# Graph layer on one core: second layer of the inner pairs in split products with the weights standing, ring of six rounds

## The reference

```python
def reference(x, src, dst, edge_attr_128, W1, b1, W2, b2):
    h = jnp.maximum(_layernorm(x, axis=-1), 0.0)
    # edge features are summed by node; the sums and h are concatenated
    agg = jax.ops.segment_sum(edge_attr_128, dst, num_segments=6250)
    z = jnp.concatenate([agg, h], axis=1)           # 6250 x 256
    hidden = jax.nn.relu(z @ W1 + b1)               # W1: 256 x 512
    return x + hidden @ W2 + b2                     # W2: 512 x 128
```

## Time and profile before

| | us |
|---|---|
| median of 3 runs | 201.23 |
| the profiled execution | 201.16 |
| its span (first to last instruction) | 199.3 |
| PE busy | 190.6 (96%) |
| DVE busy | 131.8 (66%) |
| ACT busy | 86.5 (43%) |
| POOL busy | 43.4 (22%) |
| mean of the 16 DMA engines, over the span | 313 GB/s |

### The profile page before, as it was taken

The page is one execution under the profiler, slowest core; times in us unless marked ns, Lnnn a source line. Parts: engine busy times, 40 slices in busy tenths (PEclk is TensorE's granted clock), DMA queues, the critical chain, the costliest instruction groups (busy, mean ns, idle before and its releaser), DMA issues.

```text
span 199.3 us, 6821 instructions
## 1 busy us (share of the span) xinstructions
PE 190.6 (96%) x2568; PEld 163.2 (82%) x2568; DVE 131.8 (66%) x582; ACT 86.5 (43%) x188; POOL 43.4 (22%) x119
## 2 busy tenths in 40 slices
PE   7897899998999999999999999999999999999994
PEld 5586789776797898898898898898897898898894
DVE  2865775666877677678568669588487388575221
ACT  3454526433624634623714714813813704823440
POOL 6592202202211202210220220221121121220000
PEclk9999999999999999999999999999999999999999
DMA  6999999999999999999999999999999995010011
GB/s 203 382 374 378 362 373 377 375 375 377 376 377 376 375 379 383 383 392 387 381 378 388 377 385 380 376 385 378 341 376 378 311 376 167 4 53 3 0 53 44
DMA packets 44628, 62.47 MB, mean 313 GB/s; under 512 B 1822, under 2 KB 44300, under 8 KB 44594
## 3 DMA queue, kind: packets, MB, share of 16 engines
q1 hardware_dynamic: 44264, 61.66, 87.2%
q10 hardware_dynamic: 330, 0.36, 0.5%
HBM read 58.81 MB, written 3.20 MB: 311 GB/s over the span
## 4 chain that ended last, share of the span: by engine, by line
PE 79%; DMA 15%; SPq 2%; DVE 1%; issue 1%; DVEq 0%
PE bank L867 21%; PE bank L938 20%; PE bank L907 17%; PE bank L917 15%; DMA edges<-in_edge_attr 15%; PE bank L882 3%; PE bank L891 2%; SPq L303 1%; SPq L297 1%; DVE aggT L623 1%; DVE w_lo L642 0%; PE bank L860 0%; SPq L306 0%; PE bank L837 0%; SPq L327 0%
## 5 line engine op out<-in xcount | busy, mean ns | idle before, releaser
L867 PE MATMUL bank<-edges,onehot 128*32 128x128 f32 x1656 | 52.2, 275 | 2.7 <-DMA edges<-in_edge_attr 1.6
L867 PEld LDWEIGHTS bank<-edges,onehot 128*32 128x32 f32 x1656 | 43.1, 110 | 10.2 <-issue 6.2
L623 DVE TENSOR_TENSOR aggT<-bank,aggT 128x32 f32 x277 | 35.7, 190 | 22.2 <-issue 10.2
L458 ACT ACTIVATE hidden<-bank,b_col 128x512 f32<-128x512 f32 (+2 forms) x56 | 34.2, 634 | 35.9 <-PE bank L917 35.8
L938 PE MATMUL bank<-w,hidden 128*128 128x128 f32 (+1 forms) x392 | 47.6, 278 | 0.0
L938 PEld LDWEIGHTS bank<-w,hidden 128*128 128x128 f32 (+1 forms) x392 | 45.1, 191 | 2.2 <-issue 2.0
L426 ACT ACTIVATE xn<-xs,shift,rstd 128x128 f32<-128x128 f32 (+1 forms) x49 | 21.5, 485 | 49.7 <-POOL shift L383 49.6
L375 POOL TENSOR_SCALAR var<-meanvar 128x2 f32<-128x2 f32 (+1 forms) x25 | 7.9, 317 | 127.4 <-DVE meanvar L559 127.4
L539 DVE TENSOR_TENSOR onehot<-relT,iota 128x384 f32<-128x384 f32 x69 | 34.6, 550 | 0.0
L917 PE MATMUL bank<-agg_hi,w_hi 128*128 128x512 f32 (+2 forms) x56 | 21.5, 385 | 1.4 <-DVE agg_lo L583 1.4
L907 PE MATMUL bank<-hT_hi,w_hi 128*128 128x512 f32 (+2 forms) x56 | 22.2, 396 | 0.3 <-DVE hT_lo L576 0.3
(11 more groups left out here) (104 smaller groups left out, 178.6 us busy)
## 6 DMA issues: line engine op xcount, KB each, us to landing
edges<-in_edge_attr SPq DMA_DIRECT2D x69, 768.0 KB, 10.9
xs<-in_x SPq DMA_DIRECT2D x21, 128.0 KB, 9.8
out_rows<-xs SPq DMA_DIRECT2D x10, 256.0 KB
w<-in_L_gnn_W SPq DMA_DIRECT2D x3, 256.0 KB, 10.5
out_rows<-xs SPq DMA_DIRECT2D x4, 128.0 KB
xs<-in_x SPq DMA_DIRECT2D x1, 256.0 KB, 5.8
hidden<-in_dst SPq DMA_DIRECT2D x1, 192.0 KB, 2.8
hidden<-in_dst ACTq DMA_DIRECT2D x1, 192.0 KB, 4.5
```

Of the source, the lines that this page charges most:

```text
L458: nc.scalar.activation(hidden[:, t, 0:cols], hidden_of(s, t), ACT.Relu, bias=b1_col[:, t:t + 1]).then_inc(hidden_ready, 1)
L623: nc.vector.tensor_tensor(win, turn_ps[:, at:at + W], win, ALU.add).then_inc(agg_added, 1)
L867: ins = nc.tensor.matmul(sums_ps[t * W:(t + 1) * W, cols], onehot[:, hots, e, :], edges[:, slot, e * F:(e + 1) * F], start=(g == 0), stop= ...
```

## The change

Layer 2 of the inner pairs (groups 3 to 12) becomes three fp32r products of 512 columns for each t, with W2 standing (`w2_hi`, `w2_lo`) and the hidden tile moving, also split in two (`hid_hi`, `hid_lo`). ACT makes two passes over each t (`relu_split`): full precision into a two-slot buffer (`full`, the old `w1`) and rounded into `hid_hi`; DVE subtracts (`rest_of_hidden`). The result stands turned in PSUM; ACT copies it out with b2 as its bias (`out_copy`), PE turns it back with four transposes in the next odd step (`turn_out`), and `finish` adds it to x there. The order of DVE's and ACT's steps from k = 5 on is rewritten, `add_b2` goes from steps 4 to 23, the ring has six buffers instead of eight, and the one-hot ring seven. Group 13 and the three single blocks keep the old layer 2.

```diff
-RING = 8
-HOTS = 8
+RING = 6
+HOTS = 7
...
-        ended = blocks_of(g)[-1] + 3
+        ended = blocks_of(g)[-1] + (3 if g < ONES else 4)
...
-            load(6)
             sp.dma_start(w2[:, :, :], W2.rearrange("(t p) f -> p t f", p=P)).then_inc(w2_landed, 16)
-            load(7)
...
+            def relu_split(n, s):
...
+                for t in range(HT):
+                    act.wait_ge(hidden_summed, n * HT + t + 1)
+                    if t == 0:
+                        act.wait_ge(out_summed, n)
+                    if n > ONES or t >= 2:
+                        act.wait_ge(hidden_lo_ready, (n - ONES) * HT + t - 1)
+                    nc.scalar.activation(full[:, t % 2, :], hid_ps[t][:, :], ACT.Relu, bias=bias_col[:, t:t + 1])
+                    nc.scalar.activation(hid_hi[:, t, :], hid_ps[t][:, :], ACT.Relu,
+                                         bias=bias_col[:, t:t + 1]).then_inc(hidden_ready, 1)
+
+            def out_copy(n):
+                act.wait_ge(out_summed, n + 1)
+                nc.scalar.activation(outT[:, :], out_ps[:, :], ACT.Identity,
+                                     bias=bias_col[:, HT:HT + 1]).then_inc(outT_ready, 1)
...
+                elif one is not None:
                     h_out(k)
-                if not early:
                     copy_sums(k)
-                round_agg(k - 1, chunks_by(k - 1), place(k - 1), group_of(k - 1))
...
+                    round_agg(k - 1, chunks_by(k - 1), place(k - 1), group_of(k - 1))
+                    h_out(k + 1)
+                    relu_split(one, one)
+                else:
                     copy_sums(k)
-                if k + 2 < NB:
-                    normalise(k + 2)
+                    if k + 1 < NB:
+                        normalise(k + 1)
+                    round_agg(k - 1, chunks_by(k - 1), place(k - 1), group_of(k - 1))
+                    out_copy(two)
+                    if k + 2 < NB:
+                        normalise(k + 2)
...
+            def rest_of_hidden(n, t):
+                dve.wait_ge(hidden_ready, n * HT + t + 1)
+                nc.vector.tensor_tensor(hid_lo[:, t, :], full[:, t % 2, :], hid_hi[:, t, :].bitcast(F32),
+                                        ALU.subtract).then_inc(hidden_lo_ready, 1)
...
+                if k <= EARLY + 1 or one is not None:
...
+                    if k <= ONES:
+                        add_b2(k - 1)
+                    if one is not None and one > ONES and k > EARLY + 1:
+                        finish(one - 1, one - 1)
+                else:
+                    add_sums(k - 1, bases)
+                    if k + 2 < NB:
+                        stats(k + 2)
+                    builds = ROUNDS[k + 1] if k + 1 < NB else []
+                    for t in range(HT):
+                        rest_of_hidden(two, t)
+                        if t < len(builds):
+                            build(builds[t])
+                        if t == 2:
+                            rest_of_h(k)
+                    rest_of_agg(k - 1, k - 1, place(k - 1))
+                    if k == NB - 1:
+                        add_b2(NB - 2)
...
+            def layer2_split(n):
+
+                pe.wait_ge(out_added, n)
+                for t in range(HT):
+                    pe.wait_ge(hidden_lo_ready, (n - ONES) * HT + t + 1)
+                    for i, (wt, v) in enumerate(((w2_hi, hid_hi), (w2_hi, hid_lo), (w2_lo, hid_hi))):
+                        ins = nc.tensor.matmul(out_ps[:, :], wt[:, t, :], v[:, t, :], start=(t == 0 and i == 0),
+                                               stop=(t == HT - 1 and i == 2))
+                ins.then_inc(out_summed, 1)
+
+            def turn_out(n):
+
+                pe.wait_ge(outT_ready, n - ONES + 1)
+                for j in range(2 * BLOCK // P):
+                    ins = nc.tensor.transpose(out_ps[:, j * F:(j + 1) * F], outT[:, j * P:(j + 1) * P], ident[:, :])
+                ins.then_inc(out_turned, 1)
...
+                elif one is not None:
+                    sum_rounds(k)
+                    if one != ONES:
+                        turn_out(one - 1)
+                        layer1_h(one, one)
+                    turn_sums(k)
+                    turn_x(k + 1)
+                    layer1_agg(one, one, blocks_of(one)[-1] + 1)
                 else:
                     sum_rounds(k)
                     if k == FLAG + 1:
                         pe.wait_ge(over_read, 1)
-                    if two is not None:
-                        layer2(two, two)
-                    if one is not None and one != ONES:
-                        layer1_h(one, one)
+                    if two == ONES:
+                        pe.wait_ge(w2_ready, 1)
+                    layer2_split(two)
                     turn_sums(k)
```

More of the change, by code:

```diff
@@ L693, in _ @@
                     dve.wait_ge(agg_cleared, CLEARS)
[L694 to L717, removed]
@@ L718, in _ @@
-                if 2 <= k < NB - 1:
-                    for r in ROUNDS[k + 1]:
-                        build(r)
-                if k + 2 < NB:
-                    stats(k + 2)
-                add_b2(k - 1)
+                one, two = group1(k), group2(k)
+                if k <= EARLY + 1 or one is not None:
+                    add_sums(k - 1, bases)
+                    if k == 1:
+                        rest_of_w1(0)
+                    if k >= 3:
+                        rest_of_h(k)
+                    rest_of_agg(k - 1, k - 1, place(k - 1))
+                    if k == 1:
+                        rest_of_h(2)
+                    if 2 <= k <= EARLY:
+                        finish(two, two)
+                    if k == 1:
+                        build(6)
+                        dve.wait_ge(rel_turned, 3)
+                        dve.wait_ge(bases_turned, 2)
+                        turned_cd(rel_copied)
+                        nc.vector.tensor_scalar(base_tab[:, P:FULL], row_ps[0:1, P:FULL], 0.0, float(N - 1), ALU.max,
+                                                ALU.min).then_inc(bases_ready, 1)
+                        nc.vector.tensor_scalar(base_tab[:, FULL:FULL + 1], colD[:, 0:1], 0.0, float(N - 1), ALU.max,
+                                                ALU.min).then_inc(bases_ready, 1)
+                        dve.wait_ge(rel_copied, 5)
+                        build(7)
+                        build(8)
+                    elif k == 2:
+                        build(9)
+                    if k >= 2:
+                        for r in ROUNDS[k + 1]:
+                            build(r)
+                    if k + 2 < NB:
[4 more added lines that the diff above has]
+                        finish(one - 1, one - 1)
+                else:
+                    add_sums(k - 1, bases)
+                    if k + 2 < NB:
+                        stats(k + 2)
+                    builds = ROUNDS[k + 1] if k + 1 < NB else []
[4 more added lines that the diff above has]
+                        if t == 2:
+                            rest_of_h(k)
+                    rest_of_agg(k - 1, k - 1, place(k - 1))
+                    if k == NB - 1:
+                        add_b2(NB - 2)
@@ L767, in _ @@
                 bases = load_bases(k)
-                if k > EARLY and group2(k) is not None:
-                    finish(group2(k), group2(k))
+                if k == EARLY + 1:
+                    finish(two, two)
+                    dve.wait_ge(w2_hi_ready, 1)
+                    nc.vector.tensor_tensor(w2_lo[:, :, :], w2[:, :, :], w2_hi[:, :, :].bitcast(F32),
+                                            ALU.subtract).then_inc(w2_ready, 1)
             add_sums(NB - 1, bases)
@@ L772, in _ @@
             add_b2(NB - 1)
+            finish(NS - 2, NS - 2)
             finish(NS - 1, NS - 1)
@@ L1026, in _ @@
                         turn_x(k + 1)
-                    if one is not None:
-                        layer1_agg(one, one, blocks_of(one)[-1] + 1)
                 if k == FLAG:
```

82 lines of the change are left out of this document (58 added, 24 removed).

## The result

| | before | after |
|---|---|---|
| median, us | 201.15 | 216.71 (215.75 to 217.04) |
| the profiled execution | 201.16 | 215.75 |
| its span | 199.3 | 214.0 |
| PE, DVE, ACT busy, us | 190.6, 131.8, 86.5 | 193.8, 149.9, 113.5 |

The ratio is 1.077, interval 1.0738 to 1.08: slower by 15.6 us. The sign and the main mechanism were right, the size was a third too small: the span grew by 14.7 us where 10.0 had been forecast.

The account below looks back on a forecast made before the run. DVE was to set the pace, 15.8 us for a pair against PE's 14.84; stages 6.1 + 3.7 - 0.1 + 0.3 = 10.0 gave span 209.3 and 211.2 us, own range 206 to 216, 8 in 10 198 to 216.

Parts of the forecast that it names:

- An interval of 18.8 behind step 19: Step 19: DVE waits for three turns behind `layer1_agg`, so the next `layer1_agg` comes after 18.8 us instead of 15.13: +3.7.
- About 15.8: Steps 7 to 17: DVE's loop for a pair, with the mean check, takes 15.8 us against PE's old 14.84.
- The ring: Edge loads: six buffers instead of eight cost 0; the rival that PE waits for edges had chance 0.02.
- DVE's wait for ACT in the even step: Ahead of `rest_of_agg(k)`: DVE waits for ACT's passes, `copy_sums`, `normalise` and `round_agg`, taken as 0.5 us, bounds 0 and 1.
- full drain: Rival, chance 0.05: each subtraction holds DVE for its full 0.69 us instead of 0.60: +3.6, 214.8 us.
- DVE keeps up: Rival, chance 0.22: PE stays the bound, DVE's round trip stays below 14.4 us: span 195.4, 197.3 us.
- 6 x 12.66 - 1.94 + 17.3 + 0.7: Steps 7 to 18: six pairs of DVE's loop, less two-round savings, plus check stretches and step 18: 92.1 us.
- the second loop: From end of sums through ACT, `rest_of_agg`, odd step, subtractions, last products, turns and sums: 15.7 us with a check, 14.5 without.
- C2: Even step: DVE's check and address reading between `rest_of_agg(k)` and the next odd step's `add_sums`; mean check 1.57 us.
- C1: Odd step: DVE's check and address reading behind builds, `stats` and `finish`, ahead of the even step's `add_sums`; mean check 1.57 us.
- PE's saving: New layer 2 at 2.9 plus four transposes at 0.44 against 3.77: 0.43 us less for a pair if PE never waits.
- The clock: Rival, chance 0.02: PE's clock falls to 1.2 GHz in step 20's waits, its next 10 us take up to twice that: 221 us.

Follow-up runs that it names:

- e3_dve_load: Kernel before plus four subtractions nobody reads on DVE in each even step from 6 on, and a ring of seven: 212.59 us, ratio 1.0525.
- g2_nocheck_order: Changed kernel without the overrun check and with the four products of the subtracted tile last: 200.80 us, ratio 0.9964.
- g3_check_first: Changed kernel with check operations of steps 6 to 17 moved ahead of `stats` (odd) or `rest_of_agg` (even): 211.43 us, ratio 1.0484.
- e4_order: Changed kernel with layer 2's eight products that need only ACT first, the four with `hid_lo` last: 216.45 us, ratio 1.0718.
- f7_nodep: Changed kernel whose middle product of layer 2 reads a ready tile, so PE doesn't wait for DVE's subtraction: 212.36 us, ratio 1.0566.

## Where the forecast was right, and the step that failed

**Right.** The bound moved from PE to a loop through DVE (DVE 33% of the chain, the check free before and worth 13 us after). An interval of 18.8 behind step 19 was asked for: 19.28. About 15.8 was asked for in a pair with two blocks of three rounds: the four of these took 16.64, 15.68, 16.04 and 16.31, mean 16.17. A subtraction was put at 0.60: they last 0.66 to 0.69 and the next operation starts 0.58 to 0.61 later. The ring at nothing: nothing. The stall sits in the new layer 2 with `rest_of_hidden` as releaser. DVE's wait for ACT in the even step came to 3.1 us where 3.0 stood; the 0.5 for each was chosen between 0 and 1, so this fit is partly luck. The rival "full drain" fell: had each subtraction held DVE for all of its 0.68 us, four and three builds would not fit in the 4.12 us that they took with `rest_of_h`. The rival "DVE keeps up" fell too, with e3_dve_load.

**The sum, stage by stage**, in the changed kernel's span of 214.0 against the 209.3 forecast:
- Start of step 7: 67.43, forecast 66.9 on the chain, which is 66.65 on this scale: +0.8. The last subtraction came 0.3 later, the last three products took 0.96 instead of 0.75 with the handover, the transposes 0.58 instead of 0.44.
- Six pairs: 95.6 instead of 92.6: +3.0. This is the step that failed: 6 x 12.66 - 1.94 + 17.3 + 0.7 took DVE's own loop for all six pairs (below).
- Behind 19: 19.28 instead of 18.8: +0.5.
- From step 21 to the end 31.7 instead of 31.2: +0.5.
That is 4.8 for a difference of 4.7. The median lies another 1.0 above the profiled execution, whose span was the shortest of its runs (214.0 to 215.2); this too wasn't in the sum.

**The pairs, term by term** (six pairs together, us, from `rest_of_agg` to `rest_of_agg` on DVE's timeline):

| | forecast | measured |
|---|---|---|
| odd step: `rest_of_agg`, builds, `stats`, `finish` | 17.7 | 17.5 |
| even step: `add_sums` | 9.6 | 10.0 |
| `stats`, four subtractions, builds, `rest_of_h` | 29.5 | 29.2 |
| wait for ACT | 3.0 | 3.1 |
| `rest_of_agg` | 2.0 | 2.0 |
| check and addresses, twelve stretches | 18.0 | 19.1 |
| odd step: `add_sums` | 8.6 | 9.1 |
| from it to `rest_of_agg` | 3.6 | 5.3 |
| sum | 92.0 | 95.2 |

Each line that holds DVE's own operations alone came within 0.5 us. The miss is three lines: from `add_sums` to `rest_of_agg` in the odd step +1.7, check and addresses +1.1, the two `add_sums` +0.9 together.

The first is the step of the forecast that failed in its mechanism. I had put 0.6 for it, as if DVE's own order set it. The six measured are 0.70, 0.87, 0.59, 0.68, 1.44 and 0.98: DVE waits there for ACT's `round_agg`, because `copy_sums` ahead of it waits for the end of PE's sums. That is the second loop. I had named it and given it 15.7 us, but then summed only the first. The chain goes through PE's last three products and its sums in five of the six pairs, and through ACT's passes and the even step's stretch C2 alone in one. The length of a pair is the longer of two loops in that pair. By the rows shown, from `rest_of_agg` at 112.49 to that at 128.32, the second took 15.83: products 0.96 and handover 0.04 instead of 0.75, sums 2.15 instead of 2.10. It holds only the odd step's stretch C1, and C1 was 1.47 to 2.15 us, mean 1.77, where I had used the mean over all, 1.57. This could have been read before: the odd steps of the kernel before have 1.46 to 2.27, mean 1.78.

The second line is a size: C1 came as before, 10.6 us for six, but C2, the even step's stretch ahead of `add_sums`, took 8.5 where the forecast's 18.0 left 7.3.

**PE's saving.** Forecast 0.43 for a pair. Without the check PE does 3.17 for layer 2, 0.58 for the transposes and 2.78 for `layer1_h` where it did 3.77 and 3.00: 0.24 saved. With the products reordered it is 0.38 in the best pairs. The twelve products, for which I had 2.9, come to 3.00 there (101.48 to 104.48 in the chain of g2_nocheck_order), where PE doesn't stand waiting at them.

**The clock.** I had given it 0.02, as a case in which PE's next 10 us behind the waits of step 20 take up to twice their time. A small form of it came: behind 2.88 us of waiting PE's clock was granted at 0.5 for about 3.3 us, 1.2 GHz instead of 2.4. The changed kernel by windows (us; busy of PE, PEld, DVE, ACT, POOL; granted clock, DMA share, GB/s):

```profile
168.00:171.30 3.30, 0.45 (x18) 0.18 (x9) 2.90 (x18) 0.02 (x1) 0.57 (x1) 1.00 0.81 264
...
172.00:174.00 2.00, 2.00 (x6) 1.36 (x5) 2.00 (x5) 2.00 (x5) 1.30 (x2) 0.50 1.06 389
174.00:175.00 1.00, 1.00 (x3) 0.64 (x3) 0.72 (x2) 1.00 (x4) 0.00 (x0) 0.50 1.05 374
175.00:176.00 1.00, 1.00 (x6) 0.82 (x6) 0.43 (x1) 0.17 (x1) 0.00 (x0) 0.90 0.94 330
```

It cost little, since most of it lay beside the subtractions that PE had to wait for anyway. g3_check_first has the same wait ahead of the same products and keeps its full clock:

```profile
167.33 0.47 PE L1040 MATMUL bank<-hid_hi,w_hi 128*128 128x512 f32 x1 [2.88 <-DVE hid_lo L682]
```

There the twelve products take 4.41 us (to 171.74 in its chain) where they took 4.64 at the lower clock, so the clock was worth 0.2 us, and the rest beyond 2.9 is waiting. The same two runs show that the wait alone doesn't decide whether the clock falls.

## What to carry to other kernels

Work moved onto an engine at 66% can make it the bound: measure its free time per round of the loop (here 1.1 us in 14.8), including address reading and semaphore waits, which no busy share counts. When two loops of nearly equal length run through the same engines, sum both for each round and take the longer; shortening one, as e4_order did, gave nothing that could be measured. And a side task that was free (the check, 0 us before) has to be priced anew when its cover is gone: 13 us here, 5.3 of them won back only by placing it elsewhere in the same step.

## What the runs showed of the hardware

- An fp32 subtraction of 128x512 takes 0.68 us on DVE and 1.28 to 1.61 us on GpSimd; while GpSimd does it, a 128x384 build on DVE takes up to 1.66 us instead of 0.55, and `add_sums`, with one input in PSUM, takes what it took.
- Three products of 512 columns take 0.70 us in a stream and 0.96 where a wait stands ahead of the first one's weight load: the first takes 0.50 instead of 0.40 and starts 0.34 ahead of the second instead of 0.23.
- Twelve addresses are read in some 1.0 us. `add_sums` starts 0.98 us behind the start of a 0.66 us operation with no semaphore wait behind it, and 1.63 behind the start of a 0.53 us operation with one; the idle times that the profile shows are 0.32 (with a second break of 0.28) and 1.10.
- The granted clock fell to 0.5 behind a wait of 2.88 us in the changed kernel and stayed full behind one of 2.88 in g3_check_first. It fell behind one of 1.66 us in e4_order and stayed full behind one of 1.64 in f7_nodep. In five of the profiled executions it also fell for some 3 us between 20 and 27 us into the span, where the changed kernel's didn't, so a single trace doesn't settle where it falls.
